# Two quantised residual blocks on one core: weight products before the second offset convolution, the grid added by a matmul, and three smaller edits

## The chip, the cores and the metric

One Trainium2 chip, one NeuronCore, one launch. The metric is the device time in microseconds (us) of one execution. A difference of under 1% can hardly be told from none here. The engines have short names in the views: PE is TensorE (matmuls), PEld its weight loads, DVE VectorE, ACT ScalarE, POOL GpSimd, and SP the engine that issues the DMAs.

## What is computed

Two blocks in a row on x, 4 x 256 x 16 x 16 in float32. The first is a deformable 3 x 3 convolution between two 1 x 1 convolutions:

```python
out = relu(group_norm(conv(x, w1)))                  # 256 -> 64 channels
om = conv(out, w_off, pad=1) + b_off                 # 27 maps: 9 x-offsets, 9 y-offsets, 9 masks
mask = sigmoid(om[:, 2 * K:])
py, px = grid_y + om[:, K:2 * K], grid_x + om[:, :K] # K = 9 taps
sampled = bilinear_sample(out, py, px) * mask
out = einsum('bckhw,ock->bohw', sampled, w2)
out = conv(relu(group_norm(out)), w3)                # 64 -> 256
x = relu(group_norm(out) + x)
```

The second quantises its input four times by the largest absolute value of the whole tensor (`scale = max|h| / 32767`, `round(h / scale) * scale`), with a 1 x 1 convolution, a depthwise 3 x 3, a full 3 x 3 and a 1 x 1 between, batch norms, and the residual at the end. Each maximum must be known before the next convolution starts.

## The kernel before, in words

The program is written engine by engine: the order of the instructions on an engine is the order of the code, and semaphores join the engines. There are no pools and no scheduler. An engine stops at the first wait that is not met, and all behind it stops too. The four images stand as two pairs `b2` = 0, 1, with the two images of a pair (`h` = 0, 1) in the lower and upper 64 partitions.

- **Start.** SP issues the input DMAs in the order first, x, pairs, x, x, woff, grid, consts, w2, wq, w3 (L326 to L336). PE runs `conv1` for each pair; its group norm goes through two small matmuls (`pair_sums`), a root on ACT, and `normalise` on ACT into `feat`, which POOL copies to `feat_flat`.
- **Offsets.** `om_step` (L398) is the offset convolution: five steps, each of two matmuls that write different halves (`p` = 0, 1) of `slot[0]`; the fifth step has one matmul only, since there are nine taps. DVE's `add_grid` (L866) takes the lower half to SBUF with bias and grid, ACT's `copy_om_rest` (L659) the upper. `om_turn` (L407) turns them on PE with `fold`, which is part of `consts_sb` and also adds the two halves. PE does the offsets of pair 0, two steps of pair 1, the turn of pair 0, and the other three steps.
- **Hats.** For each of four tiles t (two per pair) DVE makes bilinear weights: `differences`, `make_hats`, `apply_mask` (the Sigmoid mask comes from ACT's `make_mask`). For tiles 2 and 3 ACT does the middle part (`distance`, L676). `make_g` (L898) multiplies rows and columns into `g_rows[i % 3]`, i = 0 to 7 (tile and half); the last two are made in thirds.
- **Weight products.** `make_v(i)` (L432), i = 0 to 7, multiplies 64 partitions of `feat_flat` (the lower for even i, the upper for odd i) with eight taps of `w2`, 512 columns wide; `make_last_v(i)` does the ninth tap, 64 columns. ACT's `copy_v` takes them to `v_sb`. Products 0 to 3 are of pair 0, 4 to 7 of pair 1. All eight come after both offset convolutions.
- **Turns and samples.** `turn(n)` (L460) transposes a third of a `g_rows` on PE, in the order of `THIRDS` (L68), through three PSUM slots; ACT's `copy_g(n)` takes it to `g_cols`; `sample(t, first, last)` (L480) multiplies `g_cols` by `v_sb` into `acc[b2]`, 4 matmuls a tap.
- **Second and third group norm.** `eight_means`, `eight_vars` (L527, L537) are small matmuls; the variances of pair 0 lie in `acc[0]`. After them PE waits for the root (`std_ready` 5) and runs 8 fillers: matmuls on `zeros`, 512 columns, whose result is not used (`idle`, L363; counts in `IDLE`). Then `conv3(1)`.
- **Quantised part.** `spread_max` (L544) brings a maximum to all partitions, `make_scale` (L1025) makes the scale; for the second maximum DVE first handles pair 0 apart (`first_half_max`, L1019).

## Time and profile before

| | before |
|---|---|
| median of three runs | 91.73 us (91.2 to 92.01) |
| the profiled execution: its time | 92.01 us |
| the profiled execution: its span on the core | 90.2 us |
| mean granted TensorE clock | 0.977 of full |
| busy in the span: PE, DVE, ACT, POOL | 85%, 72%, 55%, 6% |
| the chain that ended last | PE 52%, DVE 29%, ACT 10% |

The span runs from the first to the last instruction; 1.8 us of the execution's time lie around it. A busy PE is not a PE at its peak: matmuls overlap, and their ends are modelled.

### The profile page before, as it was taken

The page shows a single profiled execution, that of the slowest core. Times are in us where ns is not written, and L with a number is a line of the kernel's source. Part 1 is how long each engine was busy: PE and PEld are TensorE (multiplying, and loading weights), DVE is VectorE, ACT ScalarE, POOL GpSimd, SP SyncE. Part 2 cuts the span into 40 slices and gives each one's busy share as a digit, 9 for nine tenths or more (in the row PEclk, how much of TensorE's full clock was granted, in tenths as well). Part 3 has the DMA queues.
Part 4 walks back from the last instruction along what each step waited for, and adds up shares of the span by engine and source line. Part 5 has one row for each costly group of instructions (what it writes and reads, how often), then busy time and mean ns, then how long its engine had stood idle before and what let it go on. Part 6 is the DMA issues. An engine that isn't in the chain of part 4 may idle for free.

```text
span 90.2 us, 2180 instructions
## 1 busy us (share of the span) xinstructions
PE 76.3 (85%) x895; PEld 52.5 (58%) x895; DVE 65.0 (72%) x176; ACT 49.5 (55%) x88; POOL 5.0 (6%) x10
## 2 busy tenths in 40 slices
PE   4989999995998989999999979999579877779600
PEld 1244664674896979798997963545224464555400
DVE  1125379999999599999894346299895885866850
ACT  4103374989929999995691027106653164632660
POOL 7501100000000000000004000000000000000000
PEclk9999999999999999999999997599999999999998
DMA  1999800000000000000000000000000000000076
GB/s 18 326 331 281 348 17 0 0 7 0 0 7 0 0 7 0 7 7 0 0 7 0 0 7 0 0 0 0 0 0 0 0 0 0 0 7 4 0 248 217
DMA packets 3274, 4.17 MB, mean 46 GB/s; under 512 B 256, under 2 KB 2688, under 8 KB 3264
## 3 DMA queue, kind: packets, MB, share of 16 engines
q1 hardware_dynamic: 2992, 3.76, 12.9%
q10 hardware_dynamic: 272, 0.26, 0.9%
q8 instruction: 7, 0.11, 0.5%
q14 instruction: 3, 0.02, 0.1%
HBM read 2.98 MB, written 1.05 MB: 45 GB/s over the span
## 4 chain that ended last, share of the span: by engine, by line
PE 52%; DVE 29%; ACT 10%; issue 4%; DVEq 0%; ACTq 0%
PE acc L487 15%; PE slot L474 9%; DVE g_rows L907 8%; PE slot L366 5%; PE acc L611 4%; DVE g_cols L1006 3%; PE acc L366 3%; ACT g_cols L808 3%; PE slot L402 3%; PE acc L590 3%; ACT g_cols L715 2%; PE acc L377 2%; DVE g_cols L1052 2%; PE slot L551 2%; ACT pad L772 2%
## 5 line engine op out<-in xcount | busy, mean ns | idle before, releaser
L907 DVE TENSOR_TENSOR g_rows<-hats 128x2304 f32<-128x2304 f32 (+1 forms) x12 | 20.6, 1751 | 0.1
L715 ACT ACTIVATE g_cols<-slot 128x768 f32<-128x768 f32 x24 | 17.8, 830 | 3.7 <-PE slot L474 3.7
L487 PE MATMUL acc<-g_cols,v_sb 128*64 128x128 f32 x288 | 17.7, 276 | 0.0
L366 PE MATMUL slot<-zeros 128*128 128x512 bf16 x56 | 15.3, 410 | 1.2 <-DVE zeros L827 1.2
L487 PEld LDWEIGHTS acc<-g_cols,v_sb 128*64 128x64 f32 x288 | 15.5, 137 | 1.1 <-issue 0.3
L474 PE MATMUL slot<-consts_sb,g_rows 64*128 64x64 f32 x288 | 11.8, 226 | 2.1 <-DVE g_rows L907 1.6
L474 PEld LDWEIGHTS slot<-consts_sb,g_rows 64*128 64x128 f32 x288 | 10.3, 140 | 3.9 <-DVE g_rows L907 2.6
L366 PEld LDWEIGHTS slot<-zeros 128*128 128x128 bf16 x56 | 5.6, 108 | 7.5 <-issue 2.7
L772 ACT ACTIVATE pad<-g_cols 64x256 bf16<-64x256 int8 x8 | 3.3, 418 | 5.0 <-DVE g_cols L1052 4.9
L750 ACT ACTIVATE dev_sb<-slot 128x4 f32<-128x4 f32 x2 | 0.3, 174 | 9.2 <-PE slot L532 9.2
L402 PE MATMUL slot<-feat,woff_sb 128*64 128x256 f32 x36 | 4.7, 385 | 0.0
L838 DVE BATCH_NORM_STATS2 stats<-acc 128x6 f32<-128x256 f32 x4 | 1.7, 428 | 3.4 <-PE acc L377 1.7
L646 ACT ACTIVATE std<-var,eps_sb 128x1 f32<-128x1 f32 x4 | 1.2, 299 | 5.1 <-DVE var L845 5.1
L551 PE MATMUL slot<-consts_sb,mx 128*128 128x128 f32 x7 | 1.9, 317 | 2.2 <-DVE mx L1128 1.2
L798 ACT ACTIVATE act<-raw,bn_off 128x256 f32<-128x256 f32 x4 | 2.0, 508 | 2.8 <-DVE mx L1128 2.8
L402 PEld LDWEIGHTS slot<-feat,woff_sb 128*64 128x64 f32 x36 | 2.7, 135 | 1.2
L551 PEld LDWEIGHTS slot<-consts_sb,mx 128*128 128x128 f32 x7 | 1.0, 164 | 3.8 <-DVE mx L1128 1.7
L366 PE MATMUL acc<-zeros 128*128 128x512 bf16 x8 | 2.7, 491 | 0.6 <-ACT std L755 0.6
L357 POOL TENSOR_TENSOR pegq<-consts_sb,wqb 128x576 bf16<-128x576 f32 x1 | 1.1, 1150 | 35.9 <-DVE wqb L963 35.9
L651 ACT ACTIVATE feat<-acc,gn_bias,gn_scale 128x256 f32<-128x256 f32 x4 | 2.3, 567 | 1.6 <-DVE gn_bias L854 1.6
L970 DVE BATCH_NORM_STATS2 stats<-slot 128x6 f32<-128x256 f32 x6 | 2.2, 412 | 1.1 <-PE slot L523 1.1
L876 DVE TENSOR_TENSOR hats<-omt_sb,consts_sb 128x576 f32<-128x576 f32 x4 | 3.0, 751 | 0.0
(144 smaller groups left out, 118.5 us busy)
## 6 DMA issues: line engine op xcount, KB each, us to landing
out<-g_cols SPq DMA_DIRECT2D x4, 256.0 KB, 2.4
x_sb<-x SPq DMA_DIRECT2D x3, 256.0 KB, 4.0
wq_sb<-wq SPq DMA_DIRECT2D x1, 484.5 KB, 6.3
woff_sb<-woff SPq DMA_DIRECT2D x1, 288.0 KB, 5.2
w_sb<-w SPq DMA_DIRECT2D x1, 288.0 KB, 5.6
x_sb<-x ACTq DMA_DIRECT2D x1, 256.0 KB, 3.2
w_sb<-w SPq DMA_DIRECT2D x1, 256.0 KB, 6.5
consts_sb<-consts SPq DMA_DIRECT2D x1, 232.0 KB, 5.5
```

The costliest lines, as they stand in the source:

```text
L366: nc.tensor.matmul(bank, zeros[:, 0:P], zeros[:], start=True, stop=True)
L402: mm = nc.tensor.matmul(slot[0][CB * p:CB * p + CB, BANK * b2:BANK * b2 + N], woff_sb[:, k, :], window(feat, b2, k), start=(s == 0), stop= ...
L474: mm = nc.tensor.transpose(slot[SLOT_OF[n % TURNS]][:, BANK * r + at:BANK * r + at + CB], g_rows[i % 3][rows(r), k, ROWS_Q * q:ROWS_Q * q ...
L487: mm = nc.tensor.matmul(acc[b2][rows(h), at:at + P], v_sb[:, B2 * h + b2, q, k, :], g_cols[t][h][:, NQ * k + q, :], start=(k == 0 and q == ...
L551: nc.tensor.matmul(spread_of(n, b2), mx[:, n, (b2, B2 - 1)[biased]:(b2, B2 - 1)[biased] + 1].to_broadcast([P, P]), ident, start=not biased ...
L590: mm = nc.tensor.matmul(acc[b2][rows(h), 0:N], w1q[:, CB * c:CB * c + CB], quot[:, c, b2, h, :], start=(c == 0), stop=(c == CH - 1))
L611: mm = nc.tensor.matmul(acc[b2][rows(h), 0:N], weights(k), window(pad[:, b2], h, k), start=(k == 0), stop=(k == TAPS - 1))
L715: nc.scalar.activation(dst.rearrange("p k (r n) -> p k r n", r=HALVES), src.rearrange("p r (k n) -> p k r n", k=per), ACT.Copy).then_inc(g ...
L772: nc.scalar.activation(dst, src, ACT.Copy, scale=256.0).then_inc(hi_ready, 1)
L808: nc.scalar.activation(piece, piece, ACT.Relu, bias=bn_off[:, 2 + c:3 + c]).then_inc(res_ready, 1)
L876: return tt(hats[:, t].rearrange("p h a k y -> p h (a k) y"), omt_sb[:, t // NQ, t % NQ, :, 0:2 * TAPS].unsqueeze(3).to_broadcast([P, HALV ...
L907: tt(g_rows[i % 3][:, taps], hats[:, t, h, 1, taps].unsqueeze(3).to_broadcast(shape), hats[:, t, h, 0, taps].unsqueeze(2).to_broadcast(sha ...
```

## The change

1. ACT loads the Sigmoid table between the root and the normalisation of pair 1, where it was loaded after the first offset copy.
2. The grid is added on PE: a tenth matmul `fold` x `grid_sb` in the free place of the fifth offset step. `grid_sb` has 128 partitions, the upper half cleared by DVE at the start. ACT copies all 128 partitions of the offsets with the bias (Identity); DVE has no part in it.
3. PE's order: offsets of pair 0, product 0, turn of pair 0, products 1 to 3, all last-tap products, products 4 and 5, offsets of pair 1, turn(0), product 6, turn of pair 1, product 7, turn(1) and on. Before the first offset convolution PE waits for woff, grid and consts. The first six thirds of g_rows 0 and 1 interleave. The last-tap products go to `slot[1]`, the turned offsets of a pair to `slot[1 - b2]`.
4. DVE's six small batch-norm operations move from ahead of the offsets to after the last mask; `differences(2)` goes behind `make_g(3)`.
5. Variances of pair 0 go to `small[0]`; the wait for the root goes; of the 8 fillers 2 stand ahead of `eight_vars(0)` and 6 behind it.
6. The second maximum of pair 0 and 1 lie side by side and are reduced in one operation of 256 columns; 1 filler between the two spreads where there were 3. `zeros` is 128 columns wide, read four times over.

```diff
-THIRDS = tuple((i, j) for i in range(WHOLE) for j in range(TURNS)) + tuple(
+THIRDS = ((0, 0), (0, 1), (1, 0), (1, 1), (0, 2), (1, 2)) + tuple(
+    (i, j) for i in range(HALVES, WHOLE) for j in range(TURNS)) + tuple(
     (WHOLE + h, j) for j in range(TURNS) for h in range(HALVES))
...
+        def omt_of(b2):
+            return slot[1 - b2][:, 0:NQ * CB]
+        def last_v_of(h):
+            return slot[1][:, BANK * h:BANK * h + T * CB]
...
-            return acc[0][:, 0:4] if b2 == 0 else slot[1][:, BANK:BANK + 4]
+            return small[0][:, 16:20] if b2 == 0 else slot[1][:, BANK:BANK + 4]
...
+                    else:
+                        mm = nc.tensor.matmul(slot[0][CB * p:CB * p + CB, BANK * b2:BANK * b2 + N],
+                                              fold, grid_sb[:, N * b2:N * b2 + N], start=False, stop=True)
...
-                pe.wait_ge(om_rest_ready, b2 + 1)
...
+            pe.wait_ge(grid_in, 16)
+            pe.wait_ge(grid_zero, 1)
+            pe.wait_ge(consts_in, 16)
+            om(0)
...
-            for i in range(4):
+            make_v(0)
+            om_turn(0)
+            pe.wait_ge(gn_ready, 4)
+            for i in range(1, 4):
                 make_v(i)
-            om_turn(1)
-            for i in range(4):
-                make_last_v(i)
-            for i in range(4, 2 * T):
-                make_v(i)
+            pe.wait_ge(omt_ready, 1)
+            pe.wait_ge(flat_ready, B2)
+            for i in range(2 * T):
                 mm = make_last_v(i)
             mm.then_inc(v_done, 1)
+            make_v(4)
+            make_v(5)
+            om(1)
...
-            turns(0, 5)
-            sample(0, 0, 4)
+            turn(0)
+            make_v(6)
+            om_turn(1)
+            make_v(7)
+            turn(1)
+            pe.wait_ge(omt_ready, 2)
+            turns(2, 3)
+            sample(0, 0, 2)
+            turns(4, 5)
+            sample(0, 3, 5)
             turns(6, 8)
-            sample(0, 5, 6)
+            sample(0, 6, 6)
...
+            idle(2, acc[0])
             eight_vars(0)
-            pe.wait_ge(std_ready, 5)
-            idle(IDLE[4], acc[0])
+            idle(6, acc[0])
             conv3(1)
...
             root(2, 1)
+            nc.scalar.preload_act_table(ACT.Sigmoid)
             normalise(2, 1, inner(feat, 1), image(acc[1][:, 0:N]), feat_ready)
...
-            copy_om_rest(0)
-            nc.scalar.preload_act_table(ACT.Sigmoid)
-            make_mask(0)
-            copy_om_rest(1)
-            for i in range(2 * T):
+            copy_om(0)
+            copy_v(0)
+            make_mask(0)
+            for i in range(1, 4):
                 copy_v(i)
...
-            add_grid(0)
-
-            dve.wait_ge(bn_std_ready, 1)
-            settle(nc.vector.reciprocal(bn_std[:], bn_std[:]))
...
-            first_half_max(2, q_floor[:, 0:1])
-            make_scale(2, first_scale[:, 2:3])
+            make_scale(2, q_floor[:, 0:1])
```

On PE, where the offsets, the weight products (L440 before, L456 after), the last-tap products (L446, L462) and the turns of the offsets (L413, L425) stand, before:

```order
L402 MATMUL slot<-feat,woff_sb 64x256 x13
L413 MATMUL slot<-consts_sb,om_sb 128x64 x2
L402 MATMUL slot<-feat,woff_sb 64x256 x5
L440 MATMUL slot<-w_sb,feat_flat 128x512 x2
L440 MATMUL acc<-w_sb,feat_flat 128x512 x2
L413 MATMUL slot<-consts_sb,om_sb 128x64 x2
L446 MATMUL slot<-w_sb,feat_flat 128x64 x4
L440 MATMUL slot<-w_sb,feat_flat 128x512
L446 MATMUL slot<-w_sb,feat_flat 128x64
L440 MATMUL slot<-w_sb,feat_flat 128x512
L446 MATMUL slot<-w_sb,feat_flat 128x64
L440 MATMUL acc<-w_sb,feat_flat 128x512
```

and of the change, from the same place:

```order
L412 MATMUL slot<-feat,woff_sb 64x256 x9
L416 MATMUL slot<-grid_sb,consts_sb 64x256
L456 MATMUL slot<-w_sb,feat_flat 128x512
L425 MATMUL slot<-consts_sb,om_sb 128x64 x2
L456 MATMUL slot<-w_sb,feat_flat 128x512
L456 MATMUL acc<-w_sb,feat_flat 128x512 x2
L462 MATMUL slot<-w_sb,feat_flat 128x64 x8
L456 MATMUL slot<-w_sb,feat_flat 128x512 x2
L412 MATMUL slot<-feat,woff_sb 64x256 x9
L416 MATMUL slot<-grid_sb,consts_sb 64x256
L494 MATMUL slot<-consts_sb,g_rows 128x64 x12
L456 MATMUL acc<-w_sb,feat_flat 128x512
```

The first product stands ahead of the first turn of the offsets, six stand ahead of the second offset convolution, and the seventh behind the first turn of a third (L494).

The same engine right behind that place, from the first turns to the samples (L487 before, L507 after) that use them, before:

```order
L474 MATMUL slot<-consts_sb,g_rows 128x64 x72
L487 MATMUL acc<-g_cols,v_sb 64x128 x20
L474 MATMUL slot<-consts_sb,g_rows 128x64 x36
L487 MATMUL acc<-g_cols,v_sb 64x128 x8
L474 MATMUL slot<-consts_sb,g_rows 128x64 x36
```

and of the change:

```order
L494 MATMUL slot<-consts_sb,g_rows 128x64 x12
L456 MATMUL acc<-w_sb,feat_flat 128x512
L425 MATMUL slot<-consts_sb,om_sb 128x64 x2
L456 MATMUL acc<-w_sb,feat_flat 128x512
L494 MATMUL slot<-consts_sb,g_rows 128x64 x36
L507 MATMUL acc<-g_cols,v_sb 64x128 x12
L494 MATMUL slot<-consts_sb,g_rows 128x64 x24
L507 MATMUL acc<-g_cols,v_sb 64x128 x12
L494 MATMUL slot<-consts_sb,g_rows 128x64 x36
```

The second turn of the offsets, with products 6 and 7 on either side of it, has moved between turn 0 and turn 1, and three taps are sampled after four turns where five were sampled after six.

On PE again, around the third group norm of pair 0 (L531 to L534 and L540 are its small matmuls, L366 the fillers), before:

```order
L531 MATMUL slot<-mv,consts_sb 128x4
L532 MATMUL slot<-mv,consts_sb 128x4
L534 MATMUL acc<-mv,consts_sb 128x4
L384 MATMUL slot<-mv,pairs_sb 128x2
L385 MATMUL slot<-mv,pairs_sb 128x1
L540 MATMUL acc<-dev_sb,consts_sb 128x4
L366 MATMUL acc<-zeros 128x512 x8
L523 MATMUL acc<-feat,w_sb 128x256 x2
```

and of the change:

```order
L559 MATMUL slot<-mv,consts_sb 128x4
L560 MATMUL slot<-mv,consts_sb 128x4
L563 MATMUL slot<-mv,consts_sb 128x4
L394 MATMUL slot<-mv,pairs_sb 128x2
L395 MATMUL slot<-mv,pairs_sb 128x1
L375 MATMUL acc<-zeros 128x512 x2
L572 MATMUL slot<-dev_sb,consts_sb 128x4
L375 MATMUL acc<-zeros 128x512 x6
L551 MATMUL acc<-feat,w_sb 128x256 x2
```

The number of fillers is the same; two of them now stand where PE waits for the squares of the deviations.

## Rows read from the trace of the kernel before

**Rows 1.** The page: span, and the chain that ended last, by engine.
```profile
span 90.2 us, 2180 instructions
PE 52%; DVE 29%; ACT 10%; issue 4%; DVEq 0%; ACTq 0%
```

**Rows 2.** Timeline (start, us, engine, line, operation), PE: offsets and products.
```profile
9.05 3.24 PE L402 MATMUL slot<-feat,woff_sb 128*64 128x256 f32 x26
12.22 0.66 PE L413 MATMUL slot<-consts_sb,om_sb 128*128 128x64 f32 x4
...
14.25 1.13 PE L440 MATMUL slot<-w_sb,feat_flat 64*128 64x512 f32 x4
15.21 1.02 PE L440 MATMUL acc<-w_sb,feat_flat 64*128 64x512 f32 x4
```

**Rows 3.** Timeline, SP: issue of consts; DMA view: time from issue to landing.
```profile
4.22 0.58 SPq L333 DMA_DIRECT2D consts_sb<-consts  x1
consts_sb<-consts SPq DMA_DIRECT2D x1, 232.0 KB, 5.5
```

**Rows 4.** Timeline, DVE and ACT around the offsets of pair 0.
```profile
11.46 0.38 ACT L662 ACTIVATE om_sb<-slot 64x256 f32<-64x256 f32 x1 [0.56 <-PE slot L402]
11.97 0.16 DVE L915 RECIPROCAL bn_std<-bn_std 128x4 f32<-128x4 f32 x1
...
13.01 0.17 DVE L921 TENSOR_SCALAR bn_minus<-bn_off 128x2 f32<-128x2 f32 x1
13.21 0.29 DVE L924 COPY omt_sb<-slot 128x128 f32<-128x128 f32 x1
15.20 0.47 DVE L869 SCALAR_TENSOR_TENSOR om_sb<-slot,first_sb,grid_sb 64x256 f32<-64x256 f32 x1
16.07 5.03 DVE L907 TENSOR_TENSOR g_rows<-hats 128x2304 f32<-128x2304 f32 x2
```

**Rows 5.** Timeline, ACT: a table load and what follows it.
```profile
34.00 1.28 ACT L724 ACT_TABLE_LOAD   x1
35.30 2.22 ACT L715 ACTIVATE g_cols<-slot 128x768 f32<-128x768 f32 x3
```

**Rows 6.** Timeline, ACT, PE and DVE from the first copies to the fifth g_rows.
```profile
20.94 4.36 ACT L715 ACTIVATE g_cols<-slot 128x768 f32<-128x768 f32 x6
23.95 2.40 PE L487 MATMUL acc<-g_cols,v_sb 128*64 128x128 f32 x40
26.29 1.34 PE L474 MATMUL slot<-consts_sb,g_rows 64*128 64x64 f32 x36
26.91 2.22 ACT L715 ACTIVATE g_cols<-slot 128x768 f32<-128x768 f32 x3 [1.61 <-PE slot L474]
30.54 0.46 DVE L894 TENSOR_TENSOR hats<-hats,mask 128x288 f32<-128x288 f32 x1 [0.89 <-ACT hats L682]
...
33.65 1.34 PE L474 MATMUL slot<-consts_sb,g_rows 64*128 64x64 f32 x36 [0.42 <-DVE g_rows L907]
```

**Rows 7.** Timeline: third group norm of pair 0 and conv3 of pair 1.
```profile
54.28 2.65 PE L366 MATMUL acc<-zeros 128*128 128x512 bf16 x8 [0.64 <-ACT std L755]
54.63 0.56 ACT L651 ACTIVATE feat<-acc,gn_bias,gn_scale 128x256 f32<-128x256 f32 x1 [0.40 <-DVE gn_bias L854]
55.26 1.47 ACT L738 ACTIVATE g_cols<-slot,gn_bias,gn_scale 128x256 f32<-128x256 f32 x3
56.87 1.23 PE L523 MATMUL acc<-feat,w_sb 64*128 64x256 f32 x4
58.14 0.76 DVE L970 BATCH_NORM_STATS2 stats<-acc 128x6 f32<-128x256 f32 x2 [2.34 <-PE acc L523]
```

**Rows 8.** Windows (us; busy PE, PEld, DVE, ACT, POOL; granted clock; DMA share; GB/s).
```profile
54.00:55.00 1.00, 0.71 (x4) 0.36 (x5) 0.82 (x7) 0.60 (x3) 0.00 (x0) 1.00 0.00 0
56.00:57.00 1.00, 1.00 (x5) 0.17 (x3) 0.00 (x0) 0.73 (x2) 0.00 (x0) 0.50 0.00 0
```

**Rows 9.** Timeline, DVE: the second maximum's scale.
```profile
70.71 0.35 DVE L1028 CUSTOM_DVE_ANT_0 unused<-slot,zero_sb,first_scale 128x128 f32<-128x128 f32 x1 [0.16 <-PE slot L551]
```

More of the change, by code:

```diff
@@ L178, in build @@
         raw = sb("raw", [P, B2, N])
-        zeros = sb("zeros", [P, BANK], BF16)
+        zeros = sb("zeros", [P, P], BF16)
         zero_sb = sb("zero_sb", [P, 1])
@@ L307, in spread_of @@
         def spread_of(n, b2):
-            return small[b2][:, P:2 * P]
+            return small[0][:, P + P * b2:2 * P + P * b2]
         def last_out(c, b2):
@@ L365, in idle @@
                 for _ in range(n):
-                    nc.tensor.matmul(bank, zeros[:, 0:P], zeros[:], start=True, stop=True)
+                    nc.tensor.matmul(bank.rearrange("p (r n) -> p r n", n=P), zeros[:],
+                                     zeros[:].unsqueeze(1).to_broadcast([P, BANK // P, P]), start=True, stop=True)
             spare = slot[1][:, BANK:2 * BANK]
@@ L417, in _, with om @@
             pe.wait_ge(woff_in, 16)
-            for b2 in range(B2):
+            def om(b2):
                 pe.wait_ge(feat_ready, b2 + 1)
@@ L531, in eight_means @@
                 nc.tensor.matmul(small[b2][:, 8:12], avg8, mv[:, b2, :, 0], start=True, stop=True)
-                nc.tensor.matmul(small[b2][:, 12:16], dev8, mv[:, b2, :, 0], start=True, stop=True
-                                 ).then_inc(sums_done, 1)
-                nc.tensor.matmul(vars_of(b2), avg8, mv[:, b2, :, 1], start=True, stop=False,
-                                 skip_group_check=True)
+                mm = nc.tensor.matmul(small[b2][:, 12:16], dev8, mv[:, b2, :, 0], start=True, stop=True)
+                if b2 == 1:
+                    mm.then_inc(sums_done, 1)
+                mm = nc.tensor.matmul(vars_of(b2), avg8, mv[:, b2, :, 1], start=True, stop=False,
+                                      skip_group_check=True)
+                if b2 == 0:
+                    mm.then_inc(sums_done, 1)
             def eight_vars(b2):
@@ L719, in _ @@
                 copy_g(n)
+                if n == 0:
+                    copy_v(6)
+                    copy_omt(1)
+                if n == 3:
+                    copy_v(7)
+                if n == 5:
+                    make_mask(1)
                 if n == 8:
@@ L904, in make_g @@
                 if i >= 3:
-                    dve.wait_ge(turned, TURNS * (i - 2))
+                    dve.wait_ge(turned, THIRDS.index((i - 3, TURNS - 1)) + 1)
                 tt(g_rows[i % 3][:, taps], hats[:, t, h, 1, taps].unsqueeze(3).to_broadcast(shape),
                    hats[:, t, h, 0, taps].unsqueeze(2).to_broadcast(shape), ALU.mult).then_inc(g_ready, 1)
-            dve.wait_ge(grid_in, 16)
             dve.wait_ge(consts_in, 16)
-            add_grid(0)
+            dve.wait_ge(omt_done, 1)
+            nc.vector.tensor_copy(omt_sb[:, 0].rearrange("p q h o -> p (q h o)"), omt_of(0)
+                                  ).then_inc(omt_ready, 1)
+            settle(differences(0))
+            make_hats(0)
+            apply_mask(0)
+            make_g(0)
+            make_g(1)
+            settle(differences(1))
+            make_hats(1)
+            apply_mask(1)
+            make_g(2)
+            make_g(3)
+            differences(2).then_inc(diff_ready, 1)
+            differences(3).then_inc(diff_ready, 1)
+            apply_mask(2)
+            make_g(4)
+            make_g(5)
+            apply_mask(3)
             dve.wait_ge(bn_std_ready, 1)
```

86 lines of the change are left out of this document (30 added, 56 removed).

## The prediction

> **What bounds the kernel now.** I read the page's chain first, then the timeline engine by engine. The chain changes hands all the time [rows 1]: no engine bounds the kernel, dependences do. The change touches three stretches, and each has its own limit.
>
> From 9.05 to 20.4 PE works without a gap: 13 offset matmuls until the first turn of the offsets at 12.22, the other five, then the weight products [rows 2]. DVE is the second limit there. It clears six batch-norm operations until 13.2, then takes the turned offsets, then spends 0.4 on pair 1's grid add (15.20 to 15.60), and makes g_rows from 16.07 [rows 4].
>
> From 21 to 33.6 the limit alternates. ACT copies six thirds (20.94 to 25.3) and idles 1.61 for PE, whose five taps (23.95 to 26.35) stand ahead of the next turns. The three copies from 26.91 and the absolute value and ramp of tile 2 behind them free DVE at 30.54, and DVE's fifth g_rows frees PE at 33.65 [rows 6]. What moves ACT's copy at 26.91 moves 33.65. From there PE is all but continuous to 52.1, so the samples end where 33.65 puts them.
>
> At the third group norm PE waits 0.64 for the root and then runs its 8 fillers, 54.28 to 56.93, while the granted clock falls from 2.4 to 1.2 GHz: 1.00 in 54 to 55, 0.50 in 56 to 57 [rows 7, 8]. `conv3(1)` could have started at 55.19, when ACT's normalised pair was ready. It starts at 56.87, behind the fillers, and DVE waits 2.34 for it [rows 7].
>
> **The change, part by part.**
>
> *The wait for consts.* The load is issued at 4.22 and lands 5.5 later, at 9.72 [rows 3]. Before, the offsets of pair 0 started at 9.05 to 9.12 [rows 2] and only the turn at 12.22 needed consts. Now the first offset step does, though what uses `fold` is the last of five. PE starts 0.65 to 0.7 later, at 9.8. The extra grid matmul is free: 13 matmuls in 3.17 [rows 2] are seven places of 0.45, so the fifth step cost a full place with one matmul in it.
>
> *Products alone.* Products of a lower and an upper half run side by side: 0 and 1 start at 14.25, 2 and 3 at 15.21 [rows 2], so a pair costs 0.96 and eight 3.84. No row has one alone. Below: 0.48, if a product only ever needs half a pair's time; above: 0.96. The offset step with one matmul took a place as long as those with two, so I take 0.9. In the new order 1 and 2, and 4 and 5, are neighbours; 0, 6 and 7 stand alone among turns of all 128 partitions, and 3 overlaps only with last-tap products. That is 2 x 0.96 + 3 x 0.9 + 0.6 to 0.9 = 5.2 to 5.5, so 1.4 to 1.7 more PE time before turn(1).
>
> *DVE's part.* Against this DVE loses the batch-norm block and both grid adds. But the turned offsets now come at 13.6 (9.8 + 2.2 offsets + 0.9 product 0 + 0.6 turn, +0.1) where it took them at 13.21; the 0.4 of pair 1's add cancels that, and g_rows start at 16.2 against 16.07. The six operations (11.97 to 13.2, 1.2 in all [rows 4]) go where the thirds of g_rows 6 and 7 are ready more than 1 us ahead of PE. I cost them at 0.05; without that cover they cost 1.2.
>
> *The walk.* I laid the rows' durations end to end in the new order (a turn 0.43, a tap 0.47, a copy of a third 0.72, a product's copy 0.55). The same walk in the old order puts the fifth g_rows' turns at 33.69 against 33.65 in the trace. New: offsets 9.8 to 12.0, product 0 to 12.9, turn to 13.5, products 1 to 3 and the last taps to 16.0, 4 and 5 to 17.0, offsets of pair 1 to 19.2, turn(0), product 6, turn, product 7 to 22.0, turns 1 to 3 to 23.3. ACT's third copy, from 22.6 on, lands at 24.1; taps 0 to 2 run to 25.5, turns 4 and 5 to 26.4, taps 3 to 5 to 27.8. ACT's copies start at 28.4 instead of 26.91, DVE's mask at 32.1 instead of 30.54, the fifth g_rows' turns at 35.2 instead of 33.65. **Early stretch: +1.5**, and the samples' end with it. With a product alone at 0.48 the same walk gives 0.0, at 0.7 it gives +0.7, at 0.96 +1.7: these are the ends.
>
> *The table load* now stands ahead of pair 1's normalisation. In the trace a load takes 1.28 and the next copy starts 1.30 after it did [rows 5]. The normalisation ends at 11.65 instead of 10.91, before the offsets of pair 0 are done at 12.0: nothing. [...]
>
> *Fillers and the root's wait.* The variances no longer lie in `acc[0]`, so six fillers follow the variance matmul at once, at about 54.0 on the old time scale. At 2.4 GHz they take 1.28 and end at 55.3, just after the normalised pair. `conv3(1)` starts 1.6 earlier than 56.87. If the clock also holds, its matmuls (1.23 for the first pair at half clock [rows 7]) take about half, and the second pair starts when ACT's second piece is read, 56.2: another 0.5. **Third norm: -2.1.** Why should the clock hold: before, PE had only matmuls of 1 to 4 columns from 52.06 to 53.6, then nothing until 54.28, before it fell; now two fillers stand among them and no gap follows.
>
> [...]
>
> *The second maximum.* The reduction grows from 128 to 256 columns: 0.35 [rows 9] plus about 0.13. PE's second spread no longer waits behind a third filler, about 0.2 to 0.25 earlier. **-0.1.** The narrower `zeros` starts the first fillers 0.2 earlier, but conv1 waits for x: nothing.
>
> **Sum:** +1.5 - 2.1 - 0.1 = -0.7. The profiled execution took 92.01 (span 90.2 and 1.81 around it), 0.28 above the median of three, so the forecast is 91.3 against 92.01 and 91.73.
>
> **Rivals.** *Products alone are cheap.* The early stretch is then 0.0 to +0.5, and the time 92.01 - 2.2 + 0.0 to 0.5 = 89.8 to 90.3. For it: 0.48 is what one costs in the old order. Against it: the lone offset matmul. Chance 0.17.
>
> *The clock falls all the same, and earlier.* If it falls while the six fillers run, they take 2.6 instead of 1.28, `conv3(1)` starts only some 0.3 earlier, and the early loss stands: 92.01 + 1.5 - 0.4 = 93.1, slower. It decides once the gain at the third norm is under 0.6. For it: PE is still thin for a microsecond and a half there, and the gap in front of the offsets at 9.1 is a new place to lose the clock. Against it: the two fillers that now stand in the thin place. Chance 0.17.
>
> *The clock falls at conv3 or later.* The fillers end in time and only the matmuls are slow: -1.6 instead of -2.1, 91.8. Chance 0.13.
>
> [...] Chance 0.03.
>
> **How the numbers follow.** The forecast as summed has 0.5, with its own range 90.7 to 91.9 (products alone from 0.8 to 0.96, the third norm 0.3 either way). The range for all is 90.0 to 93.0, which cuts the outer parts of the first two rivals. Faster by over 1% means below 90.8: the first rival and a small part of the forecast, 0.24. Slower by over 1% means above 92.65: the second rival and a little more, 0.2. Within 1%, which is about what a measurement of this kernel can't tell from nothing: 0.56.
>
> **What would show it.** PE's first offset matmul at 9.8 and not 9.1 (the wait for consts). Products 0, 6 and 7 with 0.9 each from their start to the next matmul (if 0.5, the first rival). ACT's seventh copy of a third at 28.4, the fifth g_rows' turns at 35.2, the samples' end 1.5 later than 52.1. The six fillers at 0.21 each and a granted clock of 1.00 throughout, `conv3(1)` within 0.1 of its normalised input, and DVE's statistics after it 2.1 earlier against the samples' end. I am wrong if the early stretch doesn't lose, or if the clock falls at the same place.

## The result and the profile after

The kernel after the change takes 92.48 us in the median (91.88 to 93.17, 20 executions), the kernel before 91.9 on the same chip. The ratio is 1.0075 with a 95% interval of 1.0046 to 1.0104: slower by 0.7 us, where the prediction had it faster by 0.4 against the median and 0.7 against its own profile. The time lies in the range, and the sign is wrong. All ratios here leave out executions more than 1.5% above the fastest of their kernel, so a rare loss weighs less in them than its count says.

The page of the kernel after: span, granted clock over 40 slices, the chain that ended last by engine. [rows 1] is its counterpart.

```profile
span 90.7 us, 2181 instructions
...
PEclk9999999999999999999999999999999999999996
...
PE 53%; DVE 19%; ACT 13%; DMA 6%; issue 3%; SPq 2%; DVEq 0%; ACTq 0%
```

DVE's share of the chain fell from 29% to 19%. That was no gain. In the kernel before DVE's hats and first two g_rows stand in the chain from 13.5 to 21.1; in the kernel after PE's products and offsets stand there, and DMA's 6% is the landing of x at the start. The profiled execution took 92.54.

The timeline of PE after the change, from the end of the second group norm (L395) to the turns that wait for the fifth g_rows (start, us, engine, line, operation). L412 and L416 are the offsets, L456 the products, L425 the turn of the offsets, L494 the turns of thirds, L507 samples. [rows 2, 6] answer to it.

```profile
9.52 0.36 PE L395 MATMUL slot<-mv,pairs_sb 128*128 128x1 f32 x2
10.01 2.13 PE L412 MATMUL slot<-feat,woff_sb 128*64 128x256 f32 x17
...
12.31 1.12 PE L456 MATMUL slot<-w_sb,feat_flat 64*128 64x512 f32 x2
13.37 0.66 PE L425 MATMUL slot<-consts_sb,om_sb 128*128 128x64 f32 x4
...
17.62 2.16 PE L412 MATMUL slot<-feat,woff_sb 128*64 128x256 f32 x17
...
19.93 0.59 PE L494 MATMUL slot<-consts_sb,g_rows 64*128 64x64 f32 x12
20.36 1.07 PE L456 MATMUL acc<-w_sb,feat_flat 64*128 64x512 f32 x2
21.36 0.66 PE L425 MATMUL slot<-consts_sb,om_sb 128*128 128x64 f32 x4
21.95 0.69 PE L456 MATMUL acc<-w_sb,feat_flat 64*128 64x512 f32 x1
...
22.91 1.14 PEld L494 LDWEIGHTS slot<-consts_sb,g_rows 64*128 64x128 f32 x31 [0.29 <-issue]
...
25.04 1.53 PE L507 MATMUL acc<-g_cols,v_sb 128*64 128x128 f32 x24 [0.85 <-ACT g_cols L745]
...
36.22 0.97 PE L494 MATMUL slot<-consts_sb,g_rows 64*128 64x64 f32 x24 [0.42 <-DVE g_rows L938]
```

Product 0 alone holds PE from 12.31 to the turn at 13.37, 1.06 us; product 6 alone from 20.36 to 21.36, 1.00. That is more than the 0.96 that two cost side by side in [rows 2]. Product 7 starts at 21.95; the first few matmuls of turn(1) run beside it, and the other weights of that turn are loaded from 22.91 on, 0.96 later. The fifth g_rows' turns stand at 36.22 where [rows 6] have 33.65.

The third group norm after the change, samples' end first (54.57 is the first of its small matmuls, 51.99 before). L375 are the fillers, L551 `conv3(1)`. The last line is the window 56 to 57 (us; busy PE, PEld, DVE, ACT, POOL; granted clock; DMA share; GB/s). [rows 7, 8] answer.

```profile
54.57 0.38 PE L559 MATMUL slot<-mv,consts_sb 128*128 128x4 f32 x2
...
56.43 1.46 PE L375 MATMUL acc<-zeros 128*128 128x512 bf16 x6
...
57.83 0.70 PE L551 MATMUL acc<-feat,w_sb 64*128 64x256 f32 x4
...
58.59 0.76 DVE L998 BATCH_NORM_STATS2 stats<-acc 128x6 f32<-128x256 f32 x2 [0.20 <-PE acc L551]
```

```profile
56.00:57.00 1.00, 1.00 (x8) 0.61 (x6) 0.63 (x5) 0.51 (x2) 0.00 (x0) 1.00 0.00 0
```

The granted clock stays at 1.00, `conv3(1)` starts right when its input is normalised (57.22 + 0.57), and DVE's statistics come 4.02 after the samples' end, where the profile of before has 58.14 - 51.99 = 6.15. This stretch did what was forecast against that profile. What the prediction writes as 2.4 and 1.2 GHz stands in the traces like this: fillers of 512 columns start 0.22 apart at a granted clock of 1.00 (before from 54.28 to 54.94; the six above by (1.46 - 0.38) / 5, so six cost 1.3) and 0.43 apart at 0.50 (before from 55.45 to 56.30), 2.4 and 1.2 columns a nanosecond.

So that all kernels can be compared, I cut each profiled execution into four: the **start** (first offset matmul), the **walk** (from there to the first small matmul of the third norm, which is the samples' end), the **norm** (from there to DVE's statistics of conv3) and the **rest** of the execution's time. All are read from the timelines as above. The labels are those of the experiments below.

| kernel | start | walk | norm | rest | sum |
|---|---|---|---|---|---|
| before | 9.05 | 42.94 | 6.15 | 33.87 | 92.01 |
| before, profiled again (e9) | 9.51 | 42.95 | 4.87 | 33.87 | 91.20 |
| after | 10.01 | 44.56 | 4.02 | 33.95 | 92.54 |
| e1, third norm alone | 10.21 | 42.94 | 4.01 | 34.04 | 91.20 |
| e11, third norm and second maximum | 9.20 | 42.94 | 4.01 | 33.95 | 90.10 |
| e2, after with the old third norm | 9.81 | 44.56 | 6.30 | 33.83 | 94.50 |
| e3, after with late waits | 9.69 | 44.54 | 4.01 | 33.97 | 92.21 |
| e4, products 6 and 7 together | 9.89 | 43.67 | 4.01 | 33.99 | 91.56 |
| e5, all products in pairs | 9.99 | 43.09 | 4.01 | 33.97 | 91.06 |
| e12, e5 with the table load moved back | 9.93 | 43.09 | 4.00 | 33.97 | 90.99 |
| e6, grid and table, old order | 10.01 | 43.45 | 4.87 | 33.88 | 92.21 |
| e7, all but the order of the products | 9.99 | 43.46 | 4.00 | 34.00 | 91.45 |
| e10, e7 with the table load moved back | 10.00 | 42.97 | 4.00 | 33.96 | 90.93 |
| e8, e1 without the eight fillers | 9.34 | 42.94 | 4.13 | 34.83 | 91.24 |

The walk is the same to 0.02 us wherever its code is the same (before in both profiles, e1, e11 and e8 at 42.94 or 42.95; after, e2 and e3 at 44.54 to 44.56). The start is not: 9.05 to 10.21, and kernels with the same code ahead of it (before and e1) differ by over 1 us.

### The profile page after: what moved, and what is told of

It is laid out like the page before. It is cut to its first block, busy times and chain, and to the rows that moved or that the text cites. A ratio compares the mean times of both kernels' runs of the same rounds, so it can differ in the third digit from the quotient of the medians.

```text
span 90.7 us, 2181 instructions
## 1 busy us (share of the span) xinstructions
PE 77.0 (85%) x897; PEld 51.9 (57%) x897; DVE 64.6 (71%) x173; ACT 50.3 (55%) x88; POOL 5.0 (6%) x10
## 3 DMA queue, kind: packets, MB, share of 16 engines
HBM read 2.98 MB, written 1.05 MB: 44 GB/s over the span
## 4 chain that ended last, share of the span: by engine, by line
PE 53%; DVE 19%; ACT 13%; DMA 6%; issue 3%; SPq 2%; DVEq 0%; ACTq 0%
PE acc L507 15%; PE slot L494 9%; DMA x_sb<-x 6%; PE slot L412 5%; ACT g_cols L745 4%; PE acc L643 4%; PE slot L456 3%; DVE g_cols L1037 3%; DVE g_rows L938 3%; ACT g_cols L845 3%; PE acc L622 3%; PE acc L456 2%; PE slot L551 2%; DVE g_cols L1078 2%; ACT pad L809 2%
## 5 line engine op out<-in xcount | busy, mean ns | idle before, releaser
L507 PE MATMUL acc<-g_cols,v_sb 128*64 128x128 f32 x288 | 18.0, 276 | 1.2 <-ACT g_cols L745 1.2
L507 PEld LDWEIGHTS acc<-g_cols,v_sb 128*64 128x64 f32 x288 | 15.5, 137 | 2.5 <-ACT g_cols L745 1.6
L375 PE MATMUL slot<-zeros 128*128 128x512 bf16 x54 | 14.9, 411 | 1.0 <-DVE zeros L864 1.0
L494 PE MATMUL slot<-consts_sb,g_rows 64*128 64x64 f32 x288 | 12.3, 227 | 0.6 <-DVE g_rows L938 0.4
L494 PEld LDWEIGHTS slot<-consts_sb,g_rows 64*128 64x128 f32 x288 | 10.4, 139 | 3.1 <-issue 2.4
L375 PEld LDWEIGHTS slot<-zeros 128*128 128x128 bf16 x54 | 5.5, 109 | 6.9 <-issue 2.1
L412 PE MATMUL slot<-feat,woff_sb 128*64 128x256 f32 x36 | 4.7, 383 | 0.1
L456 PE MATMUL acc<-w_sb,feat_flat 64*128 64x512 f32 x8 | 4.2, 622 | 0.0
L412 PEld LDWEIGHTS slot<-feat,woff_sb 128*64 128x64 f32 x36 | 2.9, 136 | 1.9 <-issue 0.9
L456 PE MATMUL slot<-w_sb,feat_flat 64*128 64x512 f32 x8 | 3.7, 629 | 0.0
L925 DVE TENSOR_TENSOR hats<-hats,mask 128x288 f32<-128x288 f32 x4 | 1.8, 457 | 2.1 <-ACT hats L714 2.0
L366 POOL TENSOR_TENSOR pegq<-consts_sb,wqb 128x576 bf16<-128x576 f32 x1 | 1.1, 1148 | 37.8 <-DVE wqb L991 37.8
L845 ACT ACTIVATE g_cols<-g_cols,bn_off 128x512 f32<-128x512 f32 (+1 forms) x4 | 2.5, 668 | 0.9 <-DVE g_cols L1167 0.9
```

The source lines that it names most:

```text
L375: nc.tensor.matmul(bank.rearrange("p (r n) -> p r n", n=P), zeros[:], zeros[:].unsqueeze(1).to_broadcast([P, BANK // P, P]), start=True, s ...
L412: mm = nc.tensor.matmul(slot[0][CB * p:CB * p + CB, BANK * b2:BANK * b2 + N], woff_sb[:, k, :], window(feat, b2, k), start=(s == 0), stop= ...
L456: nc.tensor.matmul(v_banks[i % 4], lhs, w2_sb[rows(h), 0:BANK], start=True, stop=True).then_inc(v_done, 1)
L494: mm = nc.tensor.transpose(slot[SLOT_OF[n % TURNS]][:, BANK * r + at:BANK * r + at + CB], g_rows[i % 3][rows(r), k, ROWS_Q * q:ROWS_Q * q ...
L507: mm = nc.tensor.matmul(acc[b2][rows(h), at:at + P], v_sb[:, B2 * h + b2, q, k, :], g_cols[t][h][:, NQ * k + q, :], start=(k == 0 and q == ...
L845: nc.scalar.activation(piece, piece, ACT.Relu, bias=bn_off[:, 2 + c:3 + c]).then_inc(res_ready, 1)
```

## The experiments

Theory A before the experiments: the products that stand alone, with the wait for consts, cost more than was summed, and the third norm gains less in most executions than in the one that was profiled. Rival B: the costs are as summed, and something else in the new order (the table load, ACT's longer copies) takes the time. The expectations name their theories anew for each run.

**e1, the edit of the third norm alone,** in the kernel before. With it, as in the change, `sums_done` is raised one matmul later, and DVE's `eight_scale(0)` waits for the root where it waited for the squares.

```diff
-            return acc[0][:, 0:4] if b2 == 0 else slot[1][:, BANK:BANK + 4]
+            return small[0][:, 16:20] if b2 == 0 else slot[1][:, BANK:BANK + 4]
...
+            idle(2, acc[0])
             eight_vars(0)
-            pe.wait_ge(std_ready, 5)
-            idle(IDLE[4], acc[0])
+            idle(6, acc[0])
...
```

> The kernel before with the third norm's edit alone: variances of pair 0 in small[0], no wait for the root, 2 fillers ahead of the variance matmul and 6 behind it. Theory A (the edit is worth 2.1 us: 1.6 because conv3 of pair 1 no longer stands behind fillers, 0.5 because the clock holds): 89.8 us against 91.9, conv3 of pair 1 at 55.3 instead of 56.87 and a granted clock of 1.00 there. Rival B (the fall of the clock in the one profile of before was an odd execution, and in most of them the fillers end by 56.0): only 0.6 to 0.9 faster, about 91.1.

Measured: 90.88 us, ratio 0.9868 (0.9812 to 0.9924, 4 executions). The norm takes 4.01, the walk is untouched. The gain is 1.2 us (0.7 to 1.7 by the interval), not 2.1. Timeline of PE at its start:

```profile
4.29 1.98 PE L377 MATMUL acc<-x_sb,first_sb 128*64 128x256 f32 x8
```

The same eight matmuls of conv1 took 1.10 in the profile of before; the offsets start at 10.21 here against 9.05. This was the first sign that the profile of before might be of an unusual execution.

**e2, the kernel after with the old third norm:** the same edit taken back.

```diff
...
-            idle(2, acc[0])
             eight_vars(0)
-            idle(6, acc[0])
+            pe.wait_ge(std_ready, 5)
+            idle(8, acc[0])
...
```

> The changed kernel with the third norm as it was before (variances in acc[0], wait for the root, 8 fillers behind it). Theory A: slower than the changed kernel by what the edit is worth, 2.1 us, 94.5. Rival B: by 0.6 to 0.9 only, 93.2. In both the samples end 2.5 us later than in the kernel before.

Measured: 94.5 us, ratio 1.0238 (1.016 to 1.0316, 4 executions), 1.5 to 2 us slower than the kernel after. Three of its four executions show a mean clock of 0.973 to 0.976, so the fall of the clock is common here. PE and DVE at its third norm, and the window 58 to 59:

```profile
56.66 2.81 PE L375 MATMUL acc<-zeros 128*128 128x512 bf16 x8 [0.64 <-ACT std L788]
59.40 1.23 PE L551 MATMUL acc<-feat,w_sb 64*128 64x256 f32 x4
...
60.67 0.76 DVE L994 BATCH_NORM_STATS2 stats<-acc 128x6 f32<-128x256 f32 x2 [2.50 <-PE acc L551]
```

```profile
58.00:59.00 1.00, 1.00 (x4) 0.28 (x2) 0.17 (x1) 1.00 (x3) 0.00 (x0) 0.50 0.00 0
```

It is the picture of [rows 7, 8]: the wait for the root, slow fillers (eight in 2.81), a granted clock of 0.50. The same edit is thus worth 1.2 in one kernel and 1.5 to 2 in the other. The profiles point to the fall as the difference: without the edit the norm takes 6.30 here, and 6.15 and 4.87 in the two profiles of the kernel before.

**e9, the kernel before once more,** unchanged, for a second profile.

> The kernel before, unchanged, once more with a profile. Theory A (a fast start and a fall of the clock at the third norm came together in the one execution profiled before, and are rare): here conv1's first eight matmuls take nearer 1.9 us than 1.1, the offsets start at 9.7 to 10.2 instead of 9.05, the clock is 0.98 or more, the fillers take under 2.0 instead of 2.65, and the samples end at 52.6 or later instead of 52.0. Theory B (the first profile is typical): offsets at 9.05, fillers 2.65, clock 0.977.

Measured: 91.69 us, ratio 0.9998 (0.9958 to 1.0039); the profiled execution 91.2, clock 0.987. Its third norm, and the window 56 to 57:

```profile
54.97 1.67 PE L366 MATMUL acc<-zeros 128*128 128x512 bf16 x7 [0.86 <-ACT std L755]
...
56.58 0.70 PE L523 MATMUL acc<-feat,w_sb 64*128 64x256 f32 x4
...
57.33 0.76 DVE L970 BATCH_NORM_STATS2 stats<-acc 128x6 f32<-128x256 f32 x2 [1.06 <-PE acc L523]
```

```profile
56.00:57.00 1.00, 1.00 (x7) 0.50 (x7) 0.27 (x1) 1.00 (x3) 0.00 (x0) 1.00 0.00 0
```

No fall: the granted clock is 1.00, the first piece of `conv3(1)` takes 0.70 and not 1.23, and the norm takes 4.87, not 6.15. Of this the edit can take only 0.86 (4.87 - 4.01). It is the part in which `conv3(1)` stands behind the fillers: its input is ready at 55.66, and it starts at 56.58. Over all executions of the kernel before in the three sessions of experiments (this run's with them) the mean clock was 0.971 to 0.980 in 16 and 0.986 or more in 59; the means of the two groups are 92.53 and 91.55. That the 16 are those with the fall at the third norm is inferred: the first profile of before shows it at 0.977 (an execution outside the 75), this one its absence at 0.987, and the distance of the group means, 0.98, is near the 1.28 between the two norms. None of the 20 executions of the kernel after lay below 0.983. Theory A expected this profile to start late as well. It starts at 9.51, between the others, with conv1's eight matmuls at 1.46: that half of the theory failed. The early start and the fall are two things, and only the fall is plainly the exception.

**e3, the kernel after with the waits for grid and consts right ahead of the grid's matmul** instead of ahead of the offsets.

```diff
-            pe.wait_ge(grid_in, 16)
-            pe.wait_ge(grid_zero, 1)
-            pe.wait_ge(consts_in, 16)
             om(0)
...
                     else:
+                        if b2 == 0:
+                            pe.wait_ge(grid_in, 16)
+                            pe.wait_ge(grid_zero, 1)
+                            pe.wait_ge(consts_in, 16)
                         mm = nc.tensor.matmul(
```

> The changed kernel with the waits for grid, its cleared half and consts moved from ahead of the first offset step to right ahead of the grid matmul in the fifth. Theory A (the wait held the first offset step by 0.6 to 0.9 us, and PE is the limit from there to turn 1): 0.5 to 0.7 faster than the changed kernel where x lands early, nothing where x lands late, so 92.0. Rival C (the start is bound by the landing of x, which came at 7.83 us in the profile of the change): no difference, 92.5.

Measured: 92.22 us, ratio 1.0025 (0.9988 to 1.0062), 0.3 to 0.5 faster than the kernel after, with the same walk; the two intervals overlap (1.0046 to 1.0104 for the kernel after). PE ahead of the offsets in e3:

```profile
9.39 0.36 PE L395 MATMUL slot<-mv,pairs_sb 128*128 128x1 f32 x2
9.69 1.08 PE L412 MATMUL slot<-feat,woff_sb 128*64 128x256 f32 x8
```

From the last small matmul to the offsets it takes 0.30 here, and 0.49 in the profile of after (9.52 to 10.01). In that execution the wait for consts thus cost 0.2, not the 0.65 to 0.75 that I summed from the early start of the profile of before: usually the offsets are not ready before 9.5 to 10 anyway. In e2 and e4, which have the early waits too, the same distance is 0.29: their consts landed at 9.41 and 9.12, and the wait cost nothing. So the profiles give the wait 0 to 0.2.

**e4, products 6 and 7 side by side.**

```diff
             turn(0)
             make_v(6)
-            om_turn(1)
             make_v(7)
+            om_turn(1)
             turn(1)
```

> The changed kernel with products 6 and 7 side by side ahead of the turn of the offsets of pair 1, where the turn stood between them. Theory A (a product alone costs 1.0, a pair the same 1.0, and PE is the limit here): 0.9 to 1.0 faster than the changed kernel, 91.5, and the fifth g_rows' turns 1.0 earlier. Rival D (ACT's copies are the limit, the lone products only fill PE's idle time): 0.2 or less.

Measured: 91.45 us, ratio 0.9981 (0.9945 to 1.0017), 0.9 faster than the kernel after (1.0075 - 0.9981 of 91.7). PE in e4:

```profile
20.24 1.08 PE L456 MATMUL acc<-w_sb,feat_flat 64*128 64x512 f32 x4
21.24 0.66 PE L425 MATMUL slot<-consts_sb,om_sb 128*128 128x64 f32 x4
...
35.20 0.96 PE L494 MATMUL slot<-consts_sb,g_rows 64*128 64x64 f32 x24 [0.42 <-DVE g_rows L938]
```

Two products in 1.00, the price of one alone, and the walk is shorter by 0.89. This is the largest single cause. Rival D (0.2 or less) is out.

**e5, all products in pairs:** e3 and e4 together, and product 1 beside product 0.

```diff
             make_v(0)
-            om_turn(0)
             pe.wait_ge(gn_ready, 4)
-            for i in range(1, 4):
+            make_v(1)
+            om_turn(0)
+            for i in range(2, 4):
                 make_v(i)
```

> The changed kernel with the late waits of e3, products 6 and 7 side by side as in e4, and product 1 moved ahead of the first turn of the offsets, beside product 0. Theory A (a lone product costs PE what a pair costs, and PE is the limit up to turn 1): the gains of e3 and e4 add up with 0.5 for products 0 and 1, about 1.9 us faster than the changed kernel, 90.6, ratio to before 0.987. Rival E (what is left of the loss lies in the order of turns, samples and copies behind turn 1): no gain beyond e4, 91.4.

Measured: 90.89 us, ratio 0.9907 (0.9874 to 0.9941), 1.5 to 1.6 faster than the kernel after, a little less than the 1.9 expected. PE in e5, products 0 and 1 ahead of the turn of the offsets:

```profile
12.30 1.13 PE L457 MATMUL slot<-w_sb,feat_flat 64*128 64x512 f32 x4
13.36 0.66 PE L429 MATMUL slot<-consts_sb,om_sb 128*128 128x64 f32 x4
```

Two products take 1.06 where product 0 alone took 1.06. The walk is 43.09: of its 1.62 above the kernel before, lone products account for 1.47 (0.89 with 6 and 7 together, 0.58 with 0 and 1). It is still not below the old walk: without lone products the new order gains nothing on the old one. e1 alone is at 0.9868, with none of it.

**e6, the grid, the table and the batch norms in the old order.** The kernel before with the grid's matmul (late waits), ACT copying the whole offsets, the Sigmoid table ahead of pair 1's normalisation, and the batch-norm block behind the last mask.

```diff
             root(2, 1)
+            nc.scalar.preload_act_table(ACT.Sigmoid)
             normalise(2, 1, inner(feat, 1), image(acc[1][:, 0:N]), feat_ready)
...
-            copy_om_rest(0)
-            nc.scalar.preload_act_table(ACT.Sigmoid)
+            copy_om(0)
             make_mask(0)
...
-            add_grid(0)
...
-            add_grid(1)
```

> The kernel before with the edits to the offsets alone: grid by a matmul (with the waits right ahead of it), offsets copied whole by ACT with the bias, Sigmoid's table ahead of the normalisation, batch-norm operations behind the last mask; order of products, third norm and second maximum as before. Theory A (DVE is the limit behind the turned offsets, and it is relieved of 0.2 and 0.4 us ahead of the first g_rows, but ACT's copies bound the first six thirds): 0.3 to 0.6 faster than before, g_rows from 15.5 on the scale of before. Rival F (the ACT chain, which ends the stretch, is not moved): no change.

Measured: 92.32 us, ratio 1.011 (1.0041 to 1.0179, 4 executions): slower than before, and outside what either theory gave it. The walk is 43.45, 0.51 longer. One of the four, at 93.11, has a mean clock of 0.971, as the 16 of the kernel before. 

**e7** is the same with the edits of the third norm and of the second maximum, so that only the order of products and thirds is missing from the change.

> All edits of the change save the order of the weight products and thirds: the edits of e6, the third norm of e1 and the one-operation maximum. Theory A: the gains of e1 (1.2) and e6 (0.3 to 0.6) and 0.06 add up, 90.0 us, ratio 0.98; the loss of the change is then all in the order of the products. Rival F: like e1 alone, 90.8.

Measured: 91.45 us, ratio 0.996 (0.9925 to 0.9995), walk 43.46: slower than both theories had it. The norm's gain is there in full and 0.5 of it is lost in the walk. ACT, PE and DVE in e7, from the table load to the first copies of thirds (L669 the load, L662 the normalisation of pair 1, L674 the copy of the offsets, L403 the first steps of pair 1's offsets, L420 the turn of pair 0's, L726 the thirds):

```profile
10.73 1.28 ACT L669 ACT_TABLE_LOAD   x1
12.03 0.57 ACT L662 ACTIVATE feat<-acc,gn_bias,gn_scale 128x256 f32<-128x256 f32 x1
12.49 0.47 ACT L674 ACTIVATE om_sb<-slot,first_sb 128x256 f32<-128x256 f32 x1
...
12.65 1.08 PE L403 MATMUL slot<-feat,woff_sb 128*64 128x256 f32 x8 [0.28 <-ACT feat L662]
13.66 0.66 PE L420 MATMUL slot<-consts_sb,om_sb 128*128 128x64 f32 x4
...
14.44 0.29 DVE L925 COPY omt_sb<-slot 128x128 f32<-128x128 f32 x1 [3.20 <-PE slot L420]
...
22.39 2.25 ACT L726 ACTIVATE g_cols<-slot 128x768 f32<-128x768 f32 x3
```

The load stands between the root and the normalisation. In the old order the first steps of pair 1's offsets come right behind those of pair 0, and they wait for it: from 12.65 on, 0.28 of idle time on PE put down to L662.

**e10, e7 with the table load where the kernel before has it.**

```diff
             root(2, 1)
-            nc.scalar.preload_act_table(ACT.Sigmoid)
             normalise(2, 1, inner(feat, 1), image(acc[1][:, 0:N]), feat_ready)
...
             copy_om(0)
+            nc.scalar.preload_act_table(ACT.Sigmoid)
             make_mask(0)
```

> All edits but the new order of products and thirds, as in the run with the old products (0.996), and with the Sigmoid table loaded behind the first copy of the offsets, where the kernel before has it. Theory A (the load ahead of pair 1's normalisation costs 0.5 in the old order): 0.5 faster than that run, ratio 0.990 to 0.992. Theory B (the grid's matmul and ACT's whole copy cost it, the load nothing): 0.996 again.

Measured: 90.93 us, ratio 0.99 (0.9866 to 0.9934), 12 executions. The same rows in e10 (start 10.00, e7's 9.99):

```profile
11.29 0.57 ACT L662 ACTIVATE feat<-acc,gn_bias,gn_scale 128x256 f32<-128x256 f32 x1 [0.55 <-DVE gn_bias L866]
12.43 0.47 ACT L673 ACTIVATE om_sb<-slot,first_sb 128x256 f32<-128x256 f32 x1 [0.57 <-PE slot L411]
12.93 1.28 ACT L704 ACT_TABLE_LOAD   x1
...
12.22 1.03 PE L403 MATMUL slot<-feat,woff_sb 128*64 128x256 f32 x8
13.18 0.66 PE L420 MATMUL slot<-consts_sb,om_sb 128*128 128x64 f32 x4
...
13.95 0.29 DVE L925 COPY omt_sb<-slot 128x128 f32<-128x128 f32 x1 [2.70 <-PE slot L420]
...
21.90 4.36 ACT L726 ACTIVATE g_cols<-slot 128x768 f32<-128x768 f32 x6
```

PE's steps of pair 1 start 0.43 earlier, the turn of pair 0's offsets 0.48, everything from DVE's copy on 0.49, and the walk is 42.97 again. The load's place was the whole loss of e6 and e7, as Theory A had it. The walk also says that taking the grid adds and the batch norms from DVE is worth nothing (42.97 against 42.94), though DVE starts its g_rows 0.47 earlier after the offsets' start (16.55 - 10.00 against 16.07 - 9.05 in [rows 4]): ACT's first copies of thirds, behind its copies of the products, start 11.90 after the offsets' start against 11.89 before [rows 6]. They bound the stretch, and they follow the products: ACT's third pair of product copies waits 0.45 for PE in both kernels (18.36 before, 19.32 in e10), and from there ACT has no gap until the thirds.

**e12, e5 with the load moved back in the same way.**

> The version with all products side by side and the late wait for consts (0.9907), with the Sigmoid table loaded behind the first copy of the offsets. In this order pair 1's offsets come late, so the load ahead of its normalisation has cover, while behind the first copy it stands in front of the first product's copy. Theory A: no gain, 0.990 to 0.995. Theory B (the load's place costs 0.5 in every order): 0.985.

Measured: 90.58 us, ratio 0.989 (0.9837 to 0.9943). The interval holds both theories' numbers; the walk decides, and it is 43.09, as in e5. In the new order pair 1's offsets start 6.8 us behind those of pair 0 (in e5), so the load ahead of its normalisation is hidden, and the forecast's "nothing" holds for the change as it was made.

**e11, third norm and second maximum alone.**

```diff
...
-            first_half_max(2, q_floor[:, 0:1])
-            make_scale(2, first_scale[:, 2:3])
+            make_scale(2, q_floor[:, 0:1])
...
```

> The kernel before with the edit of the third norm and that of the second maximum, nothing else. The edit of the third norm alone gave 0.9868. Theory A (each edit gives what the traces show, 1.2 and 0.07 us): 0.986. Theory B (0.9868 was a lucky session with four executions): 0.990 or above.

Measured: 90.5 us, ratio 0.9888 (0.9823 to 0.9954, 6 executions). The interval holds both theories' numbers, so the time doesn't decide. The traces do, on the small term: from the last maximum's reduction to the first operation that uses the scale it takes 1.63 before it was changed (69.67 to 71.30 in the profile of before) and 1.56 in the kernel after (70.27 to 71.83). The rest is 33.95 here against 34.04 in e1.

**e8, e1 without any of the eight fillers** at the third norm, whose results nothing uses.

```diff
-            idle(2, acc[0])
             eight_vars(0)
-            idle(6, acc[0])
```

> e1 without the 8 fillers of that stage: variances in small[0], no wait for the root, nothing between the variance matmul and conv3 of pair 1. If the gain of e1 is that conv3 of pair 1 doesn't stand behind fillers, it stays in the executions at full clock. Theory A (fillers among the small matmuls keep the clock): more executions with a granted clock under 0.98, conv3 at half clock in them, 0.3 to 1 us slower than e1. Rival G (the fillers do nothing for the clock there): like e1, 90.9.

Measured: 91.74 us, ratio 0.9998 (0.9954 to 1.0042); the mean clock is 0.95 to 0.969 in all ten executions. PE in e8, and the window 56 to 58:

```profile
55.53 0.84 PE L523 MATMUL acc<-feat,w_sb 64*128 64x256 f32 x4 [1.60 <-ACT feat L653]
...
56.61 1.23 PE L523 MATMUL slot<-feat,w_sb 64*128 64x256 f32 x4 [0.24 <-ACT g_cols L740]
```

```profile
56.00:58.00 2.00, 1.76 (x9) 0.64 (x6) 1.21 (x6) 1.01 (x3) 0.00 (x0) 0.50 0.00 0
```

Without fillers PE idles 1.60 ahead of conv3, the granted clock is 0.50 from 56 to 58 and 0.66 in the next two microseconds, where e1 shows 1.00 in both. Against e1 the norm is 0.12 and the rest 0.79 longer, and by the ratios the whole gain of e1, 1.2 us, is gone. So here the fillers held the clock. Their place decides whether they stand in the way, and by the counts it may also decide how often the clock falls: a mean under 0.981 in 16 of 75 executions of before, three of four of e2 and one of four of e6, which have the old third norm, against 3 of 88 in the kernels with the new one. No run separates the place from the removed wait.

None of the kernels leaves out a part of what the reference computes. The fastest are e1, e11, e12, e10 and e5, at 0.987 to 0.991 with intervals that overlap: each beats both kernels, and e1 does it with one edit.

## Why the prediction was wrong

Two steps of the sum failed, each by nearly as much as the whole error of 1.1 (0.4 faster forecast, 0.7 slower measured). "The walk" in the early stretch was to grow by 0.8 and grew by 1.62, of which 1.47 goes when no product stands alone (e4, e5). "Third norm: -2.1" was read off one execution in which the clock fell, and the edit alone (e1) gained 1.2.

Profile against profile, the change is +0.96 at the start, +1.62 in the walk, -2.13 at the norm and +0.08 in the rest, +0.53 in all. Against the second profile of before it is +0.50, +1.61, -0.85 and +0.08, +1.34. The measured difference (+0.7 by the ratio, +0.6 by the medians) lies between them; the starts differ from execution to execution whatever the kernel.

- **What bounds the kernel: right.** The dependences that I followed are those that moved. The fifth g_rows' turns set the samples' end: 36.22 - 33.65 = 2.57 later, and the samples' end is 54.57 - 51.99 = 2.58 later.
- **"So I take 0.9" for a product alone: too small.** Products 0 and 6 cost 1.06 and 1.00, above the upper end of 0.96 that I had set, and product 7 0.96 (21.95 to 22.91). That a lone product costs as much as a pair was the right reading of the lone offset matmul; the discount from 0.96 to 0.9 had no row behind it. The three make 0.32.
- **"The walk": +0.8 after its own start forecast, +1.62 measured; profile against profile this is the largest failed step.** Besides the 0.32: each offset convolution takes 2.30 until the next work and not 2.2 (twice 0.1), the stretch from the first turn of the offsets to the end of product 5 is 4.25 and not 4.1, and turn(0), product 6, the turn of the offsets and product 7 take 2.98 (19.93 to 22.91) and not 2.8, of which 0.16 is already counted. That makes 0.7 of the 0.82; the last 0.1 comes in the taps, turns and copies behind. The whole early stretch, +1.5 with ends at 0.0 and +1.7, came out at 2.58, beyond the upper end. From the last offset matmul to product 0 it takes 0.30 (12.01 to 12.31), where the steps before take about 0.22; no run here shows what makes the difference of 0.08.
- **"The wait for consts": 0.65 to 0.75 forecast, 0.2 in the profile of after, 0 in those of e2 and e4, 0.3 to 0.5 by the ratios of e3 and after, whose intervals overlap.** I set a fixed landing of 9.72 against a start of 9.05 that no other profile reaches. The rest of the start's +0.96 is conv1, which took 1.27 and not 1.10, and x, which landed late (PE waited 0.40 for it). Whether the late x has to do with the change is open: PE waits for x there in three of the six profiles with the new kernel's start (after, e3, e5) and in none of the other eight.
- **"DVE's part" and the table load: right in the changed order, for the wrong reason.** The normalisation did not end before pair 0's offsets: it ended at 12.42, and the copy of the offsets began only then. The load still cost nothing (e5 and e12 have the same walk), but only because pair 1's offsets had been moved away; in the old order it costs 0.5. I had checked it against pair 0's copy and not against what waits for pair 1's normalisation. DVE's g_rows started at 16.74 and not 16.2, with the later offsets and product 0. ACT's copy of the offsets grew from 0.38 to 0.47, a term that the sum lacked; the new copy takes 128 partitions and a bias where the old one took 64 and none, and no run separates the two. The chance of 0.03 was for a load that costs more than [rows 5] show. No run has one: in e7 the normalisation starts 1.30 after the load did (10.73 to 12.03), as in [rows 5].
- **"Third norm: -2.1": right against the profile it was made from, wrong as a forecast of the median.** The norm went from 6.15 to 4.02. But 1.28 of it was the fall of the clock, which by their clocks some 16 of 75 executions have. Without it the edit gives 0.86. Weighted by 16 in 75 that is 0.86 + 0.21 x 1.28 = 1.1, close to e1's 1.2. The match with the profile was luck: that execution happened to be one with the fall. The text itself had the warning: the profiled execution was the slowest of three, 0.28 above their median, and I took that for noise around one mechanism instead of asking whether the mechanism was the exception.
- **"The second maximum: -0.1": 0.07.** Right. The reduction of 256 columns took 0.48 in the kernel after (from 71.11), as summed (0.35 and 0.13). But the rest is 0.17 longer with the new third norm (33.87 against 34.04 in e1), where the second piece of `conv3(1)` now waits 0.37 for ACT. I had that wait, but no price for it.
- **The rivals.** Products alone are not cheap. The clock did not fall at the fillers or at conv3 in the profile of after, and none of its 20 executions lies below 0.983: the forecast's own answer on the clock was right. The time came out on the side of the second rival (93.1), but by other terms.

The sum with the measured terms, against the mix of executions: +1.62 in the walk, 0 to +0.2 for consts by the profiles, -1.1 at the norm, about 0.1 in the rest: +0.6 to +0.8, against 0.69 measured (0.42 to 0.96 by the interval). The walk and the norm's length are shown by e1 to e5 and the profiles; the weight of the fall rests on the counts of clocks, and the starts spread by more than the remainder.

## What to carry to other kernels

Before a stall of one profile enters a sum, ask how many executions have it: the spread of times and clocks beside the profile tells, and a gain that only removes a rare fall is worth its share. Cost a matmul that uses half the rows at the price of a pair, and keep two halves neighbours when reordering: here a product on 64 partitions took 0.96 to 1.06 alone, and two side by side took the same. When work is taken from one engine, find which engine bounds the same stretch next: here DVE was relieved by half a microsecond (0.47, e10), and ACT's copies, behind PE's products, kept the end where it was.

## What had not been expected of the hardware

- **The start of an execution varies by more than the change did.** The first eight matmuls of conv1 took 1.10, 1.17, 1.27, 1.30, 1.35, 1.46, 1.68 and 1.93 to 1.98 in the profiles, and the offsets started at 9.05 to 10.21. The granted clock is shown as 1.00 there (in before, e9, e1, e12 and after, from 1 to 7 us), also while the seven fillers ahead take 3.10 to 3.17, where six take 1.46 at the third norm. Those seven start 0.43 apart in before and after alike, as at a granted clock of 0.50 above, and a matmul of conv1 lasts 0.38 to 0.43 in before and 0.63 to 0.69 in e1. My estimate from these numbers is that PE goes over to its faster pace up to 0.9 us (1.98 - 1.10) later in one execution than in another, without the clock's row showing it. What sets it stays open.
- **The fall at the third norm comes and goes with the same code** (16 of 75). It is common in e2, where the old third norm stands behind the new order (three of four), and never showed in the kernel after or in e1, e3, e4, e10, e11 and e12 (68 executions, none below 0.982). e5 and e7, which have the same third norm, show a mean clock of 0.969 and 0.975 in 1 and 2 of 10 executions; these were not profiled, and where the clock fell in them is open.
